# Decoder layer on Trainium2: projected items in halves, GpSimd's work in 512-wide pieces, and batch 0's output work moved earlier

## What is computed

```python
def bitnet_linear(x, weight, scale_param):
    s = maximum(mean(abs(weight), axis=1), 1e-8)
    y = einsum('bsi,oi->bso', x, sign(weight / s[:, None]))
    return nan_to_num(y * (s * scale_param), nan=0.0, posinf=1e6, neginf=-1e6)

h = layernorm(x)
q, k, v = (bitnet_linear(h, w, sc) for w, sc in (q, k, v))   # 32 query heads, 8 key/value heads, head_dim 16
attn = softmax(q @ k.T / 4)          # per head, 512 x 512
x = x + bitnet_linear(attn @ v, o_weight, o_scale)
W = base + mean(abs(w - base)) * sign(w - base)              # for w1, w2, w3; inner width 1792
h = layernorm(x)
out = x + (silu(h @ W1.T) * (h @ W3.T)) @ W2.T
```

## Time and profile before

| what | us |
|---|---|
| median of 3 runs | 1053.17 |
| lowest and highest | 1047.9, 1053.53 |
| the profiled execution: its own time | 1054.04 |
| its span | 1052.0 |
| busy in it: PE, DVE, ACT, POOL | 968.0, 736.5, 538.8, 293.1 |
| mean granted clock of PE, share of 2.4 GHz | 0.955 |

### The profile page before, as it was taken

How to read it: one execution, slowest core, us unless ns; L and a number is a source line. 1 busy time by engine, 2 the same in 40 slices (tenths; PEclk the granted TensorE clock), 3 DMA queues, 4 the chain that set the end, 5 groups by cost and what they waited for, 6 DMA issues and landing times.

```text
span 1052.0 us, 14162 instructions
## 1 busy us (share of the span) xinstructions
PE 968.0 (92%) x4770; PEld 617.9 (59%) x4770; DVE 736.5 (70%) x978; ACT 538.8 (51%) x999; POOL 293.1 (28%) x247
## 2 busy tenths in 40 slices
PE   3588989999999989898889999999999999999997
PEld 2433433344344433333357888888888888888886
DVE  6585867888888787789695558855687557864443
ACT  3426768877897889574684331332223232232221
POOL 3134767566766642210000110101111110011110
PEclk9858998999999999688999999999999999999999
DMA  4535577455754575511494000240003300130001
GB/s 149 149 127 171 158 150 227 127 146 174 224 153 115 170 224 161 179 45 32 151 303 151 12 1 1 80 148 17 0 0 120 124 0 0 45 116 1 0 0 40
DMA packets 81361, 110.24 MB, mean 105 GB/s; under 512 B 10144, under 2 KB 33696, under 8 KB 81312
## 3 DMA queue, kind: packets, MB, share of 16 engines
q1 hardware_dynamic: 79152, 108.04, 33.8%
q10 hardware_dynamic: 2160, 1.58, 0.5%
HBM read 76.29 MB, written 32.78 MB: 104 GB/s over the span
## 4 chain that ended last, share of the span: by engine, by line
PE 70%; DVE 14%; DMA 5%; issue 3%; ACT 3%; SPq 3%; POOL 2%; DVEq 0%; ACTq 0%; POOLq 0%
PE psum L1389 15%; PE psum L1390 15%; PE psum L1391 14%; DVE nmx L994 8%; PE psum L1308 7%; PE psum L1298 7%; PE psum L1282 3%; DMA q_slot<-shift 3%; DVE g_alt L963 2%; PE psum L1319 2%; PE psum L1320 2%; PE psum L1225 1%; PE psum L1226 1%; ACT probs L832 1%; SPq L454 1%
## 5 line engine op out<-in xcount | busy, mean ns | idle before, releaser
L994 DVE TENSOR_REDUCE nmx<-psum 128x2 f32<-128x1024 f32 x256 | 300.9, 1218 | 74.6 <-PE psum L1282 74.3
L832 ACT ACTIVATE probs<-psum 128x512 f32<-128x512 f32 x512 | 276.1, 604 | 77.1 <-PE psum L1298 74.9
L1298 PE MATMUL psum<-q_slot,k_slot 50*128 50x512 f32 x512 | 172.0, 492 | 16.9 <-DMA q_slot<-shift 13.0
L1389 PE MATMUL psum<-fxh,wh 128*128 128x512 f32 x448 | 175.2, 391 | 2.2 <-DVE wl L1152 2.2
L1390 PE MATMUL psum<-fxl,wh 128*128 128x512 f32 x448 | 174.9, 390 | 0.0
L1391 PE MATMUL psum<-fxh,wl 128*128 128x512 f32 x448 | 174.7, 390 | 0.0
L719 POOL CAST dh<-w2T 128x512 fp32r<-128x512 f32 (+1 forms) x56 | 50.7, 906 | 430.1 <-PE psum L1391 393.5
L1298 PEld LDWEIGHTS psum<-q_slot,k_slot 50*128 50x128 f32 x512 | 77.5, 193 | 132.1 <-ACT probs L832 85.6
L1308 PE MATMUL psum<-probs,v_slot 128*32 128x512 f32 x1024 | 146.4, 646 | 0.7 <-ACT probs L832 0.7
L1282 PE MATMUL psum<-k_slot,q_slot 48*128 48x512 f32 x512 | 115.3, 465 | 26.7 <-DVE nmx L994 24.8
L1159 DVE TENSOR_TENSOR gate<-gate,psum 128x512 f32<-128x512 f32 x56 | 38.4, 686 | 133.6 <-PE psum L1391 131.3
(11 more groups left out here) (109 smaller groups left out, 1272.7 us busy)
## 6 DMA issues: line engine op xcount, KB each, us to landing
stage<-in_L_ffn_mean_w_dram SPq DMA_DIRECT2D x84, 256.0 KB, 4.6
q_slot<-q_stack SPq DMA_DIRECT2D x64, 192.0 KB, 3.5
stage<-in_L_ffn_w_dram SPq DMA_DIRECT2D x42, 256.0 KB, 4.8
q_stack<-q_hi SPq DMA_DIRECT2D x32, 256.0 KB
weighted_values<-u_sb SPq DMA_DIRECT2D x32, 256.0 KB, 3.8
k_slot<-k_stack SPq DMA_DIRECT2D x64, 96.0 KB, 3.6
xn<-_attn_hidden_states_dram SPq DMA_DIRECT2D x4, 1024.0 KB, 6.8
q_stack<-q_lo SPq DMA_DIRECT2D x16, 256.0 KB
```

The costliest lines, as they stand in the source:

```text
L832: nc.scalar.activation(probs[kt][:, j, :], BANK[ring_bank(("score", g, kt, j))], ACT.Exp, scale=HEAD_DIM ** -0.5).then_inc(exp_ok, 1)
L994: v.tensor_reduce(column, pair, AX.X, ALU.max, negate=True).then_inc(s_max, 1)
L1298: mm(BANK[ring_bank(("score", g, kt, j))], k_slot[s][rows, kt * P:(kt + 1) * P], q_slot[s][rows, jj, :], start=True, stop=True).then_inc(t ...
L1389: mm(o, lhs_hi, rhs_hi, start=first, stop=False)
```

## The change

Items beside the steps are projected in two halves of 256 tokens in two steps following each other; each half is scaled by itself. The guard and the split come one step later each. GpSimd's differences and sums are done in three pieces of 512 instead of one of 1536, in three steps, and the sets of weights are due four steps later; the first two sets are loaded in groups 0 and 1. Item stores thereby fall in groups 3, 3, 4, 5, 6 of a batch instead of 2, 3, 4, 5, 5, and differences from the third on in odd groups instead of even ones. Batch 0's sums are loaded in group 21, its x, output and reciprocals in group 23, and the reciprocals taken in step 27 of batch 2; `attended` moves from steps 10 to 13 to 4 to 7 and the projections from 16, 20, 24, 28 to 11, 16, 20, 26. Before the steps, K and V come first, signs are transposed through two banks in place of four, Q's signs come between the first items, and the row sums of W_o after all guards. The order of the scores in a step stays. Core of the diff:

```diff
-GUARD_LAG, PRED_LAG = 1, 3
-VT_AT = 24
-INVERT_AT, ATTENDED_AT, PROJECT_AT, PROJECT_EVERY = 4, 10, 16, 4
-DIFF_AT = tuple(range(1, 112, 8))
-SIGN_LAG, ABS_LAG, SUM_LAG = 2, 5, 8
+GUARD_LAG, PRED_LAG = 2, 4
+VT_AT = 26
+INVERT_AT, ATTENDED_AT = 27, 4
+PROJECT_AT = (11, 16, 20, 26)
+HSEQ = SEQ // 2
+DIFF_AT = tuple(range(5, 112, 8))
+SIGN_LAG, ABS_LAG, SUM_LAG = 2, 5, 6
...
-    WEIGHT_SETS = ((QT, 4), (KTILE, 2), (OT, 4))
+    WEIGHT_SETS = ((KTILE, 2), (QT, 4), (OT, 4))
+    SIGN_ORDER = (KTILE, VTILE, QT, QT + 1, QT + 2, QT + 3, OT, OT + 1, OT + 2, OT + 3)
+    SIGN_BANK = (6, 7)
+    VT_BANK = 4
...
-            t = (at - PROJECT_AT) // PROJECT_EVERY
-            return ("project", t) if at in range(PROJECT_AT, SLICES, PROJECT_EVERY) else None
+            return ("project", PROJECT_AT.index(at)) if at in PROJECT_AT else None
         if XT_AT <= at < XT_AT + KT:
             return "xT", b, at - XT_AT
-        if at in ITEM_AT:
-            return "item", b, ITEM_AT.index(at)
+        for i in range(len(ITEMS)):
+            if 0 <= at - ITEM_AT[i] < 2:
+                return "item", b, i, at - ITEM_AT[i]
...
+        elif kind == "item" and which[2] == 0:
+            eng.wait_ge(y0_ok, NI * (which[0] - 1) + which[1] + 1)
...
-
-        for e in range(2):
-            load_difference(e)
...
+            if g < 2:
+                load_difference(g)
             for e in range(2, IT):
-                if 4 * g - 2 < DIFF_AT[e - 2] + SUM_LAG + 1 <= 4 * g + 2:
+                if 4 * g - 2 < DIFF_AT[e - 2] + SUM_LAG + 3 <= 4 * g + 2:
                     load_difference(e)
...
             if g == 3:
                 load_factors()
             if g == 5:
                 spread_factors()
-            if b == BATCH - 1 and at == 0:
+            if b == BATCH - 2 and at == SLICES - 12:
                 for p in range(2):
                     sp.wait_ge(u_out[p], 16 * KV_HEADS // 2)
                 load_sums(0)
+            if b == BATCH - 2 and at == SLICES - 4:
                 sp.wait_ge(v_ok, BATCH)
+                for i in range(2, 5):
+                    sp.wait_ge(part_out[(5 * (BATCH - 1) + i) % Q_RING], stored(BATCH - 1, i))
                 load_batch(0)
-            if b == BATCH - 1 and at == 4:
                 load_reciprocals(0)
...
+        def difference(e, k):
+
+            if k == 0:
+                pool.wait_ge(fw_in[e % 2], 96 * (e // 2 + 1))
+            nc.gpsimd.tensor_tensor(wn[e % 2][:, k, :], wn[e % 2][:, k, :], mn[e % 2][:, k, :], ALU.subtract).then_inc(fd_ok, 1)
+
+        def add_magnitude(e, k):
+
+            pool.wait_ge(fabs_ok, 3 * e + k + 1)
+            positive(pool, facc_ok, 3 * e + k - 2)
+            nc.gpsimd.tensor_tensor(dacc[:, k, :], dacc[:, k, :], mn[e % 2][:, k, :], ALU.add).then_inc(facc_ok, 1)
...
-            if kt == 2 and g + 2 < GROUPS:
+            if kt == 3 and g + 2 < GROUPS:
...
+                if 0 <= 4 * g + kt - DIFF_AT[e] < 3:
+                    difference(e, 4 * g + kt - DIFF_AT[e])
+                if 0 <= 4 * g + kt - DIFF_AT[e] - SUM_LAG < 3:
+                    add_magnitude(e, 4 * g + kt - DIFF_AT[e] - SUM_LAG)
...
-        def scale_item(b, i, bank):
+        def scale_item(b, i, bank, half=None):
             n = NI * b + i
-            act.wait_ge(q_mm, n + 1)
+            c = slice(0, SEQ) if half is None else slice(HSEQ * half, HSEQ * (half + 1))
+            if half == 0:
+                act.wait_ge(q0_mm, NI * (b - 1) + i + 1)
+            else:
+                act.wait_ge(q_mm, n + 1)
             positive(act, yg_ok, n + 1 - Y_RING)
-            nc.scalar.activation(yq[n % 2][:], BANK[bank], ACT.Copy, scale=wstat[:, 3, ITEMS[i]:ITEMS[i] + 1]).then_inc(yq_ok, 1)
+            nc.scalar.activation(yq[n % 2][:, c], BANK[bank][:, c], ACT.Copy, scale=wstat[:, 3, ITEMS[i]:ITEMS[i] + 1]
+                                 ).then_inc(y0_ok if half == 0 else yq_ok, 1)
...
+        act.wait_ge(wstat_ok, 1)
+        for m in (KTILE, VTILE):
+            sign_tile(m)
+        for m in (KTILE, VTILE):
+            signs_out(m)
         for kt in range(KT):
             act.wait_ge(xT_ok, kt + 1)
             nc.scalar.activation(xh[:, kt, :], BANK[kt], ACT.Copy).then_inc(xh_ok, 1)
-        for i in range(NI):
-            scale_item(0, i, 4 + i % 3)
-            if i > 0:
+        act.wait_ge(wstat_ok, 2)
...
+        for m in (QT, QT + 1):
+            sign_tile(m)
+        signs_out(QT)
+        act.wait_ge(oscale_ok, 1)
+        scale_item(0, 0, 4)
+        signs_out(QT + 1)
+        for m in (QT + 2, QT + 3):
+            sign_tile(m)
+        hi_item(0)
+        for m in (QT + 2, QT + 3):
+            signs_out(m)
+        for i in range(1, NI):
+            scale_item(0, i, 4 + i % 2)
+            if i > 1:
                 hi_item(i - 1)
...
         weight_scales(0)
-        weight_scales(1)
         dve.wait_ge(rstd_ok, 1)
         for t in range(TT):
             v.tensor_scalar(xn[:, t, :], xn[:, t, :], mv[:, t, 0:1], rstd[:, t:t + 1], ALU.subtract, ALU.mult).then_inc(xn_ok, 1)
-        weight_scales(2)
+        weight_scales(1)
         dve.wait_ge(scl_in, 64)
         output_scales(slice(0, OT))
-        output_scales(slice(OT, WTILES))
-        dve.wait_ge(wstat_ok, 5)
+        dve.wait_ge(oscale_ok, 1)
...
         for i in range(NI):
             guard(i)
+        weight_scales(2)
+        output_scales(slice(OT, WTILES))
...
+            if b == BATCH - 1 and at - 1 in PROJECT_AT:
+                t = PROJECT_AT.index(at - 1)
                 scale_output(0, t, ring_bank(("project", t)))
...
+            if b == BATCH - 2 and at == INVERT_AT:
+                invert_sums(0)
...
-                if PROJECT_AT <= at:
-                    t, part = divmod(at - PROJECT_AT, PROJECT_EVERY)
-                    if part == 2:
-                        guard_output(c_chain)
-                    if part == 3:
-                        add_output(0, t, c_chain)
+                if at - 2 in PROJECT_AT:
+                    guard_output(c_chain)
+                if at - 3 in PROJECT_AT:
+                    add_output(0, PROJECT_AT.index(at - 3), c_chain)
...
-            pe.wait_ge(sgn_ok, m + 1)
-            positive(pe, signs_ok, m - 3)
+            n = SIGN_ORDER.index(m)
+            pe.wait_ge(sgn_ok, n + 1)
+            positive(pe, signs_ok, n - 1)
...
-        def project_item(b, i, bank):
+        def project_item(b, i, bank, half=None):
 
             m = ITEMS[i]
             w = slice(m * P, (m + 1) * P)
+            c = slice(0, SEQ) if half is None else slice(HSEQ * half, HSEQ * (half + 1))
             for kt in range(KT):
-                mm(BANK[bank], signs[:, kt, w], xh[:, kt, :], start=(kt == 0), stop=False)
-                last = mm(BANK[bank], signs[:, kt, w], xl[:, kt, :], start=False, stop=(kt == KT - 1))
-            last.then_inc(q_mm, 1)
+                mm(BANK[bank][:, c], signs[:, kt, w], xh[:, kt, c], start=(kt == 0), stop=False)
+                last = mm(BANK[bank][:, c], signs[:, kt, w], xl[:, kt, c], start=False, stop=(kt == KT - 1))
+            last.then_inc(q0_mm if half == 0 else q_mm, 1)
...
+        first_item(0)
+        for m in (QT, QT + 1):
+            transpose_signs(m)
+        pe.wait_ge(signs_ok, 3)
+        first_item(1)
+        for m in (QT + 2, QT + 3):
+            transpose_signs(m)
+        pe.wait_ge(signs_ok, OT)
+        for i in range(2, NI):
+            first_item(i)
+        transpose_values_in(0, VT_BANK)
```

73 lines of the change are left out of this document (27 added, 46 removed).

## The result

The changed kernel takes 1076.01 us (median of 4 runs, 1074.41 to 1085.38), the one before 1050.54 us beside it: a ratio of 1.0264, 95% interval 1.0191 to 1.0338. That is 2.6% slower, 20 us over the forecast and 7 us above its range. The profiled execution took 1074.41 us for a span of 1072.5, so 20.5 us more than the profile of before.

A forecast was written before the change was run, and what follows sets the result against it. TensorE, busy 968.0 of 1052.0 us, was taken as the bound, DVE in some steps. Terms -10.5 - 8.5 + 9 + 1.3 + 1.9 + 3.8 + 3.7 + 2.4 - 1 gave +2.1: forecast 1056 us, range 1041 to 1069.

The forecast's parts named there:

- rival B: Groups 1, 3, 5 of every batch: differences beside tokens or item stores make shifts late; +12 us, 1068; chance 0.2.
- rival A: SP's queue: a small shift is not held up by what stands before it; 1040, with half 1046; chance 0.3.
- Rival C: Half items on PE: matmuls paced by their weight loads at 0.16 us; +10 us, 1066; chance 0.06.
- Rival D: Steps stay uneven, set by POOL's chain of mask and copy; the 10.5 shrinks to 4, 1062; chance 0.1.
- Items evened out: Steps of batches 0 to 2: halves and pieces win back PE's idle time, -10.5 us before the halves' cost.
- Pieces at no cost: GpSimd's 1536-wide work in 84 pieces: 11 us more on POOL in all, at no cost to the kernel.
- Batch 0's output: Groups 21 to 25: wait of 10.7 us for group 25's shift, replacing 8.8 us lost in group 25; +1.9 us.
- Projection earlier: Batch 3: three outputs' guard and add, not two, fall in steps with maxima, where DVE bounds; +3.8 us.
- Batch 0's start: Group 1's shift issued ahead of the second set of differences, its wait gone, later steps shorter; -8.5 us.
- Factors: Group 3: 2.25 MB more ahead of the factors' 2560 small writes, next shift waits longer; +9 us, bounds 0 and +12.
- Halves' price: Items on PE: a half takes 1.0 us, an item 2.0 for 1.87, over 18 items; +2.4 us.
- Before the steps: Before the first scores: item 1's store +1.3, W_o's row sums on DVE +2.4 to 2.8; +3.7 us.

The follow-up runs named there:

- a4: The changed kernel with batch 0's output (loads, inversion, attended, projection) back in batch 3: 1065.6 us, ratio 1.0158.
- f2: The changed kernel with the old grid of differences (tiles in even groups, two groups ahead), output's loads still early: 1060.5 us, ratio 1.0078.
- b1: The changed kernel with batch 0's output back in batch 3 and the old grid; early start, halves and pieces stay: 1051.4 us, ratio 1.0015.
- d4: b1 with item stores due one slice sooner and the factors stored in group 7, spread in 15: 1034.3 us, ratio 0.9845.
- a1: The changed kernel with each pair of weight tiles loaded one group later, in even groups: 1072.3 us, ratio 1.0211.
- f1: The changed kernel with each item's stores due one slice sooner (groups 2, 3, 4, 5, 5 of a batch): 1083.0 us, ratio 1.0270.
- e1: The kernel before with only the differences' grid moved by half a period, tiles in odd groups: 1084.7 us, ratio 1.0327.
- d3: The kernel before with only GpSimd's differences and sums in 512-wide pieces over three slices: 1051.8 us, ratio 0.9998.
- b3: The kernel before with only items in halves and their later guard, split and values; GpSimd's differences 1536 wide: 1073.2 us, ratio 1.0269.
- e2: The kernel before with only the loads of batch 0's output moved to groups 21 and 23, sums inverted at slice 27: 1059.4 us, ratio 1.0095.
- a3: The changed kernel with attended from slice 10 and projection at 16, 20, 24, 28 again, output's loads still early: 1070.6 us, ratio 1.0168.
- b2: The kernel before with the first two pairs of weight tiles loaded in groups 0 and 1, first difference at slice 4: 1044.4 us, ratio 0.9993.
- d2: The changed kernel with the factors stored in group 7 and spread in 15 instead of 3 and 5: 1069.3 us, ratio 1.0168.
- d1: b2 with the factors stored in group 7 and spread in 15 instead of 3 and 5: 1035.4 us, ratio 0.9853.
- e3: d4 with the load of x for batch 0's output moved from group 24 to 26: 1030.5 us, ratio 0.9816.
- c1: The changed kernel with x and the attended values loaded in group 24, behind group 25's shift, attended one slice later: 1065.7 us, ratio 1.0177.

## Why the prediction was wrong

Two of the change's parts can be set against each other in four kernels that share the halves, pieces and start:

| | output's loads early | in batch 3 |
|---|---|---|
| tiles in odd groups | 1.0264 (changed) | 1.0158 (a4) |
| tiles in even groups, two groups ahead | 1.0078 (f2) | 1.0015 (b1) |

The grid is worth 1.4 to 1.9%, 15 to 20 us; the output's early loads 0.6 to 1.1%, 7 to 11 us, each difference good to some 0.7 to 0.9%; all other parts together nothing measurable. Together they are the 25 us. The forecast had +1.9 for the output, and for the grid only what it does in groups 3, 5 and 23 (in the terms +9, +1.3 and +1.9), and rival B.

Three sums of the forecast don't come out as written: 5.3 + 2.8 at the start is 8.1, not 8.5; half of rival A's 16 us leads to 1048, not 1046; and B, C, D with a quarter of the forecast make 0.45 for slower, not 0.36. None of them moves the forecast near 1076.

- **Items evened out, -10.5: the step that failed.** I took PE's idle time of batches 1 and 2 as what better order gives back, and asked of the shifted grid and of the later stores only what they do in groups 3, 5 and 23. Measured, for -2.8 and -2.5 with the halves' price: +5.6 and +0.4. Where no shift is late (d4) the two batches are 1.5 and 1.4 us shorter than before, about half of what the terms give. In the changed kernel 4.1 of batch 1's 5.6 us are the steps at groups 12 and 13. The stores of items 0 and 1 and a pair of tiles fall together in group 3 of every batch; moving the tiles (a1, f2) or the stores (f1) takes the stall at groups 12 and 13 away, and e1 shows that the grid alone, with whole items stored in their old groups, doesn't make it. The time isn't won back with that stall alone, since others come up (a1, f1); it is with the old grid (f2, batch 1 at 103.8). This is rival B's mechanism in batch 1 (chance 0.2), and its place, group 3 of a batch, was on its list; batch 2 has it hardly, at 3.7 and 3.3 us. I argued against it that batch 1 has no such wait now, which is true of the old grid only.
- **Pieces at no cost: right in price, wrong in what they are for.** d3 is no faster than before. They pay for the halves (b3 against b1) and for the grid: with wide pieces the grid costs 3.3% (e1).
- **Batch 0's output, +1.9: the largest error of a size.** I had the wait about right (13.5 us on PE, for 10.7 worked out, bound 14) but set against it all 8.8 us that group 25 lost before. What was gained was 5.0: group 25 after the wait still took 14.2 us for 10.4, at a granted clock of 0.67, so groups 24 and 25 together rose by 9.1. I had also misread the 8.8: PE waited 1.9 us for that shift; the larger part began with DVE's wait of 4.3 us for the sums. The store went out at 410.9, not 414.1, but landed at 421.2, not 416.5. That the grid put tiles into group 23 was in the sum; without them the step is still 13.1 to 14.1 (f2, e2).
- **Projection earlier, +3.8: not borne out.** Groups 26 to 31 did take 4.6 us more, but with the work put back late (a3) they took the same, 91.2 (the ratios leave room for about 1%). In the kernels with the old grid they take 82 to 88 us (94 with halves alone), in those with the new one 90 to 101: it is the grid here too. With the output in batch 3 most of the grid's price stands here (a4 against b1, 12.4 us), it seems by the queue; with the output early it is 2.8 (changed against f2), and PE's waits for maxima are 12.4 us for 7.0. In one place of the changed kernel one sees how: at 466.3 DVE's guard runs beside GpSimd's pieces, which the old grid has elsewhere, and its instructions take 1.4 to 1.8 us for 0.7.
- **Batch 0's start, -8.5: right** (-9.0 over three steps), in b2 too.
- **Factors, +9 with a bound of 0 to 12: near in size by luck, wrong in cause.** The step rose by 6.5 us, the next one took 5.6, as before; batch 0 came out at -1.2, forecast about -1.8. But the 2.25 MB put ahead didn't make the shift later: it landed at 147.99, before at 150.44. I had PE where it was before; it came 9.2 us earlier, by the start that I had counted as -8.5. The halves' later stores alone, with the old start, leave the step at 6.5 (b3), the early start alone makes it 9.2 (b2), both together 12.6 without tiles in group 3 (b1) and 12.9 with them. With the factors gone it falls by 6 to 10 (d2, d1, d4). So the factors' store, not the 1.5 MB, holds the shift. Rival A, that a small shift isn't held up, is refuted. By the rule that I quoted from the Trainium skill (DMA: Bandwidth & Descriptors, Queues, rings and completion order) an increment waits for the earlier writes of its engine; that fits the landings in before (150.4 behind 150.0) and d2; in the changed kernel the shift was in 1.6 us before the factors (134.19 + 15.4 = 149.6), so it didn't wait for all of them. The trace shows something beside it: the issue of the two parts of the shift took 4.4 us in before and 5.1 and 7.1 us in the changed kernel and b1, 1.1 in most other places.
- **Halves' price, +2.4: right.** 0.12 us a matmul, and PE busy 101.3 and 100.9 us in b1's batches 1 and 2 for 100.3 and 100.4. Rival C is refuted.
- **Before the steps, +3.7: wrong**, -0.6; the first scores come at 51.8 us, for 52.4 before. **Tail**: the rest of the kernel came 2.8 us later where I had -1; it varies from 532.9 to 539.9 us over the profiles of the table, so no term can be read from it.
- **Rival D** (GpSimd's chain sets the steps) is seen in b3 and e1, not in the changed kernel, whose predicated copies take 0.9 us at most.

Not tried: a faster way for the factors (one contiguous store), and the odd grid with whole items and pieces, which would split the grid's price between queue and GpSimd; and halves with pieces but the old start.

## What to carry to other kernels

When a schedule constant shifts a periodic load by half a period, write down for every group what its in-order DMA queue now holds; the cost is not where the constant is used but at the small transfer behind it that the next stage waits for. Read the landing time of that transfer against the bytes ahead of it, and let only what is needed soon stand there: here 2560 small writes moved from a full group to an empty one gave 1.4% (b2 to d1), and the whole redistribution of work nothing that can be measured (b1). Ask too what an earlier start will meet: a transfer that lands at the same time as before is waited for all the longer. Halved work on one engine and finer pieces on its neighbour may lose or do nothing alone and balance only together, as halves and pieces did here (b3, d3, b1), so test them apart and together.

## What the runs showed of the hardware

- A DVE predicated copy with 0.75 us of work took 3.53 us while GpSimd subtracted two 128x1536 arrays (278.53 to 281.97), and ended 0.6 us after it: held until GpSimd was done, then run at nearly its usual length. (The kernel before has such copies too, up to 3.60 us; that the grid decides which maxima stand behind them is my reading.) The Trainium skill (SBUF — State Buffer, SBUF: two separate sides) says that a DVE instruction with two SBUF inputs and a GpSimd one that reads SBUF take the shared ports for their whole length, the later one blocked; the trace agrees. GpSimd's piece length is thereby a latency of DVE's: on the same odd grid, pieces of 3.5 us came with 1.0327 (e1), pieces of 1.3 us with 1.0158 (a4, which has halves and the early start as well).
- Behind a store of 10 KB in 4-byte elements, the next issue on SP's queue took 4.39 us (before), 5.08 us (changed) and 7.09 us (b1), 1.1 us in most other places, and the step was 6 to 10 us longer. The 10 KB say little about the price of such a store, and the place says much: it landed 13.7 us after its issue in group 7 of d1, where the next issue came 7.9 us behind it and took 1.06 us, and no step of groups 6 to 8 was above 4.4 us.
- A 64 KB store came back after 4.0, 5.2, 6.5, 8.7, 10.33 and 12.14 us (e3, c1, d4, a4, changed, f2); the two longest with 2 MB and more just ahead of it. Here the time of a round trip through DRAM followed what had been issued just ahead of it.
